# A transformer block with convolutional projections: the 3-tap convolution by minimal filtering, and a new order of the stages

## The chip, the cores and the metric

The kernel runs on one core of a Trainium2 chip. The metric is device time in microseconds. Five engines run at the same time, each on its own list of instructions in program order, and meet only at semaphores: TensorE (PE, matrix products into PSUM), VectorE (DVE), ScalarE (ACT), GpSimd (POOL, which here works on SBUF only) and SyncE (SP, which here issues nearly all DMA transfers).

## The reference, cut to what matters

The input x has 2 batches of 1024 tokens of 512 features. The block is an attention part and a feed-forward part (FFN), both with scale, shift and gate taken from a condition vector c.

```python
mod = (silu(c) @ wmod).reshape(2, 6, 1, 512)            # sa, ca, ga, sb, cb, gb
h = layernorm(x) * (1 + ca) + sa
y = conv1d(h, conv_w, taps=3, 'SAME') + conv_b          # 512 -> 3 * 128: thirds q, k, v
q, k, v = split(y, 3)                                   # in blocks of 128 tokens
qh, kh, vh = q @ wq + bq, k @ wk + bk, v @ wv + bv      # 16 heads of 64
o = softmax(causal(qh / 8 @ kh.T)) @ vh                 # within each block
x = x + ga * ((o @ wo + bo) @ proj_w + proj_b)
h = layernorm(x) * (1 + cb) + sb
x = x + gb * (h @ base_w.T + base_b + 0.5 * sum_over_top2_experts(weight * (h @ A.T) @ B))
```

The convolution for token t is g0 h[t-1] + g1 h[t] + g2 h[t+1], with g0, g1, g2 matrices of 512 x 384.

## The kernel before, in words

**Number format.** Every product runs in three passes over pairs of 16-bit halves: each operand is kept as a high half (the value rounded to float16) and a low half (what the rounding left), and PE adds high x high, high x low and low x high. So each operand that is made costs two operations: ACT writes the high half, then DVE or POOL writes the low half as value minus high half.

**Tiling.** The 2048 tokens are 8 chunks of 256 tokens (two blocks of 128). A chunk goes through these stages, named as in the list `SCHEDULE` as name:chunk:part. na and nb: mean, variance and normalisation of the input (statistics on DVE, the root in small steps on POOL, the scaling on DVE at L819). ht: PE transposes a block of 128 tokens x 512 features into a PSUM bank (L1065). hs: ACT and DVE take it out as high and low half into hT (L659, L824). halo: POOL copies the edge columns that the outer taps need from the chunk beside (L538). c: the convolution, a third (q, k or v) at a time, 36 matmuls of 256 tokens (L1167): 3 taps x 4 blocks of 128 features x 3 passes. When the last of them is done, ACT and DVE take the third out of PSUM with its bias as cv (L671, L898). qk and v: head projections (ACT L686, L697, DVE L907, L915). s: scores of 8 heads; m: their maximum on DVE (L921); e: exponential on ACT (L713); nz: normalisation on POOL (L587); ph: halves (ACT L722, DVE L927) and transposition by DMA; pv: product with v (oT on ACT L731, DVE L937). wo, pr: output projections and residual. l2a, l2b: second normalisation (xn, L970). hs2, lr, ro, rw: routing to experts. fb: base product; G and gh: routed activations (POOL L625; halves ACT L769, DVE L1020); fl: expert product and the result.

**Weights.** sp stages split weights. The convolution weights carry the factor (1 + ca), so they are split once per batch, in groups of four 128x384 operations on ACT (L647) and as many on DVE (L880): sp 0, 1, 2 for batch 0 and sp 11, 12, 13 for batch 1.

**The order.** `SCHEDULE` is one written list. Each engine walks it and issues its own part of every stage, so the list fixes the order within each engine and the waits do the rest. An instruction that waits holds back all that follow it on its engine, SP's transfers too. At the start SP issues the loads of x, of the modulation weights (wma, four parts), of the three thirds of the convolution weights (cw_raw) and of a projection weight (pw_raw), in this order on one queue. PE meanwhile computes the modulation: rp and row (L1081), its transposition cols (L1091), then vb (the convolution's bias, L1101), and then the convolution of chunk 0.

```python
tap, c, (a, b) = step // (3 * DC), step // 3 % DC, PASSES[step % 3]
ins = nc.tensor.matmul(bank_c[:, 0:CH], cw[:, i, a, c, tap, :],
                       hT[:, j % 2, b, c, OWN - 1 + tap:OWN - 1 + tap + CH],
                       start=step == 0, stop=step == STEPS - 1)
```

The same SBUF and PSUM are shared by all stages; three PSUM banks (C) serve ht, c, qk, v, pr and lr in turn.

Of the kernel before, what the change touches and what calls it, by code (L numbers as in the profile page):

```python
# [42 lines left out]
def bass_adaln_block(nc, x, cw_in, pw_in, wo_in, pj_in, bsw_in, btw_in, ar_in, small_in, pb_in, bb_in, wmod_in,  # L43
# [11 lines left out]
    STEPS = TAPS * DC * 3  # L55
    HALF = NC // 2
    S_SCALE = DH ** -0.5 / QK_SCALE ** 2
    assert W == P and D == 4 * P and 2 * DH == P and 2 * R == P and NC == 8 and CH == 2 * P
# [10 lines left out]
        hs:2:0 v:0:2 s:0:1 m:0:1 v:0:3 v:0:0 ph:0:0 c:1:3 pk:0:0 c:1:3 bias:0:0 c:1:3 ht:2:1 halo:2:0 c:1:3 e:0:1
        c:1:9 pj:0:1 nz:0:1 c:1:6 s:0:2 nb:3:0 m:0:2 c:1:3 hs:2:1 c:1:12 ph:0:1 cols:0:1 c:1:3 pk:0:1 c:1:6 e:0:2  # L70
        c:1:6 nz:0:2 c:1:15 qk:1:1 qk:1:0 xr:0:0 pv:0:0 qk:1:5 v:0:1 s:0:3 m:0:3 ph:0:2 qk:1:7 qk:1:4 c:1:3 na:4:0
        c:1:15 e:0:3 c:1:3 pick:0:2 c:1:12 nz:0:3 c:1:3 ht:3:0 hs:3:0 xr:1:0 qk:1:3 pv:0:1 qk:1:6 v:1:0 v:1:1 s:1:0
# [1259 lines left out]
```

## Time and profile before

| | us |
|---|---|
| timed runs | 458.02, 460.03, 460.16 (median 460.03) |
| profiled execution, first to last instruction (span) | 455.5 |
| median of the timed runs less that span | 4.5 |

| engine | busy us | share of the span | instructions |
|---|---|---|---|
| PE | 430.2 | 94% | 4284 |
| DVE | 364.4 | 80% | 695 |
| ACT | 303.0 | 67% | 976 |
| POOL | 250.6 | 55% | 301 |

The profile tells of one execution. Its own time is the span and what lies around it, which the profile does not show; beside the median of the timed runs that is 4.5 us. Times of instructions are from the span's start. The busy time of a pipelined engine holds the latency of the last operation of a series, so single durations (mean ns) add up to more than a series takes.

### The profile page before, as it was taken

To read this page: it belongs to the slowest core of one execution; us is meant where nothing else is said; L and a number is where in the kernel's file an instruction comes from. 1 tells how busy PE (TensorE), PEld (TensorE's weight loads), DVE (VectorE), ACT (ScalarE), POOL (GpSimd) and SP (SyncE) were. 2 spreads that over 40 slices of the span, in tenths; PEclk is the share of its full clock that TensorE was granted. 3 is DMA by queue.
4 is the path that set the end of the run, shared out by engine and by line. 5 is a ranking of instruction groups with operands and counts; after the bars stand their busy time and mean duration, and the time that the engine had idled before them with its cause. 6 is when DMAs were issued, how large, how long until landed. Compare 5 with 4: busy or idle time off the path is not lost.

```text
span 455.5 us, 11377 instructions
## 1 busy us (share of the span) xinstructions
PE 430.2 (94%) x4284; PEld 285.9 (63%) x4284; DVE 364.4 (80%) x695; ACT 303.0 (67%) x976; POOL 250.6 (55%) x301
## 2 busy tenths in 40 slices
PE   8799999999999998999999999979999898988996
PEld 6458578776887665576668765646675474454442
DVE  4879999999989899668976896568969986955751
ACT  2635888997987897566767687737777786541220
POOL 4103345321462877364675795535777779577471
PEclk9999999999999998999999999999999999999999
DMA  8994097232275298253891369353964563783642
GB/s 313 407 399 172 3 242 222 56 88 46 50 133 124 57 212 219 56 109 55 155 206 54 63 117 188 103 110 70 178 105 105 89 123 80 129 130 71 148 97 65
DMA packets 128006, 60.91 MB, mean 134 GB/s; under 512 B 117808, under 2 KB 118064, under 8 KB 127568
## 3 DMA queue, kind: packets, MB, share of 16 engines
q1 hardware_dynamic: 127808, 60.17, 56.1%
q8 instruction: 34, 0.56, 0.5%
q14 instruction: 20, 0.16, 0.1%
q10 hardware_dynamic: 144, 0.02, 0.1%
HBM read 26.63 MB, written 4.19 MB: 68 GB/s over the span
## 4 chain that ended last, share of the span: by engine, by line
PE 57%; DVE 20%; DMA 6%; POOL 6%; ACT 5%; issue 3%; SPq 2%; ACTq 0%; DVEq 0%; POOLq 0%
PE C L1167 15%; PE C L1037 12%; PE F L1037 11%; PE S L1213 4%; PE W L1230 3%; ACT prob L713 3%; PE W L1037 3%; DMA cw_raw<-in_cw_dram 3%; DVE xn L970 3%; DVE p L927 2%; PE S L1037 2%; DVE qk L907 2%; DVE nm L921 2%; DVE g L1020 2%; PE S L1205 2%
## 5 line engine op out<-in xcount | busy, mean ns | idle before, releaser
L587 POOL TENSOR_TENSOR prob<-prob,rinv 128x1024 f32<-128x1024 f32 x32 | 65.3, 2040 | 79.6 <-DVE rinv L932 79.5
L1167 PE MATMUL C<-hT,cw 128*128 128x256 f16 x864 | 108.0, 275 | 0.0
L1167 PEld LDWEIGHTS C<-hT,cw 128*128 128x128 f16 x864 | 82.4, 99 | 17.3 <-issue 2.6
L713 ACT ACTIVATE prob<-S,nms 128x128 f32<-128x128 f32 x256 | 90.1, 379 | 1.0
L1037 PE MATMUL F<-btw,gT 128*128 128x512 f16 x336 | 74.8, 379 | 0.0
L686 ACT ACTIVATE qk<-C,bqk 128x256 f16<-128x256 f32 x128 | 52.3, 481 | 21.1 <-PE C L1037 20.6
L907 DVE SCALAR_TENSOR_TENSOR qk<-C,bqk,qk 128x256 f16<-128x256 f32 x128 | 54.3, 474 | 10.5 <-ACT qk L686 10.4
L1037 PEld LDWEIGHTS F<-btw,gT 128*128 128x128 f16 x336 | 32.7, 98 | 38.0 <-DMA gT<-g 0.4
L713 ACT ACTIVATION_READ_ACCUMULATOR prob<-S,nms 128x1 f32 x256 | 55.7, 218 | 0.0
L1037 PE MATMUL C<-cv,pw 128*128 128x256 f16 x384 | 49.9, 273 | 3.5 <-DVE xb L948 3.1
L927 DVE SCALAR_TENSOR_TENSOR p<-prob,p 128x1024 f16<-128x1024 f32 x32 | 42.3, 1322 | 2.3 <-ACT p L722 2.2
L921 DVE TENSOR_REDUCE nm<-S 128x4 f32<-128x512 f32 x64 | 40.8, 678 | 3.4 <-PE S L1213 3.3
L1037 PEld LDWEIGHTS C<-cv,pw 128*128 128x128 f16 x384 | 35.9, 98 | 12.0 <-DVE xb L948 3.5
L1037 PE MATMUL F<-bsw,h 128*128 128x512 f16 x168 | 38.4, 379 | 0.9 <-DVE ob L1027 0.9
L722 ACT ACTIVATE p<-prob 128x1024 f16<-128x1024 f32 x32 | 34.0, 1062 | 2.0 <-DMA pt<-p 1.7
L625 POOL TENSOR_TENSOR G<-cmb,lr 128x1024 f32<-128x1024 f32 x15 | 30.1, 2005 | 2.0 <-DVE cmb L1011 1.7
L731 ACT ACTIVATE oT<-W 128x512 f16<-128x512 f32 x32 | 19.4, 607 | 15.2 <-PE W L1230 15.1
L1230 PE MATMUL W<-pt,v 128*64 128x128 f16 x768 | 27.5, 221 | 1.2 <-DVE oT L937 1.2
L631 POOL TENSOR_TENSOR xb<-xb,ob 128x512 f32<-128x512 f32 x12 | 16.5, 1379 | 21.8 <-DVE ob L1027 21.5
L1037 PEld LDWEIGHTS F<-bsw,h 128*128 128x128 f16 x168 | 16.0, 98 | 19.5 <-issue 1.3
L1230 PEld LDWEIGHTS W<-pt,v 128*64 128x64 f16 x768 | 22.4, 110 | 9.3 <-issue 6.8
L1213 PE MATMUL S<-qk 64*128 64x128 f16 x768 | 27.0, 217 | 0.0
(196 smaller groups left out, 756.6 us busy)
## 6 DMA issues: line engine op xcount, KB each, us to landing
xa<-in_x_dram SPq DMA_DIRECT2D x10, 512.0 KB, 4.9
xb<-in_x_dram SPq DMA_DIRECT2D x6, 512.0 KB, 4.1
wmb<-in_wmod_dram SPq DMA_DIRECT2D x1, 3072.0 KB, 19.1
out_dram<-xb SPq DMA_DIRECT2D x12, 256.0 KB, 2.5
cw_raw<-in_cw_dram SPq DMA_DIRECT2D x3, 768.0 KB, 10.6
raw<-in_cw_dram SPq DMA_DIRECT2D x3, 768.0 KB, 5.0
wma<-in_wmod_dram SPq DMA_DIRECT2D x4, 512.0 KB, 6.9
bt_raw<-in_btw_dram SPq DMA_DIRECT2D x2, 1024.0 KB, 5.7
```

The costliest lines, as they stand in the source:

```text
L587: nc.gpsimd.tensor_tensor(prob[:, i % 2], prob[:, i % 2], rinv[:, i % 2].unsqueeze(2).broadcast_to([P, 8, P]), ALU.mult).then_inc(p_normal, 1)
L625: nc.gpsimd.tensor_tensor(G_of(i), cmb[:, n].unsqueeze(2).broadcast_to([P, E, R]), lr[:, n, 0:R].unsqueeze(1).broadcast_to([P, E, R]), ALU ...
L686: nc.scalar.activation(qk16[:, HI, c], C[k][:, a * CH:(a + 1) * CH], ACT.Identity, bias=bqk[:, c:c + 1]).then_inc(c_hi, 1)
L713: ins = nc.scalar.activation(prob[:, i % 2, h], S[i % len(S)][h // 4][:, (h % 4) * P:(h % 4 + 1) * P], ACT.Exp, bias=nms[:, i % 2, h:h + 1 ...
L722: nc.scalar.activation(p16[:, HI], prob[:, i % 2], ACT.Copy, scale=P_SCALE).then_inc(p_hi, 1)
L907: ins = nc.vector.scalar_tensor_tensor(out=qk16[:, LO, c], in0=C[k][:, a * CH:(a + 1) * CH], scalar=bqk[:, c:c + 1], in1=qk16[:, HI, c], o ...
L921: ins = nc.vector.tensor_reduce(nm[:, i % 2, 4 * h:4 * h + 4], S[i % len(S)][h][:].rearrange("p (h k) -> p h k", h=4), AX.X, ALU.max, nega ...
L927: nc.vector.scalar_tensor_tensor(out=p16[:, LO], in0=prob[:, unit(j, n) % 2], scalar=P_SCALE, in1=p16[:, HI], op0=ALU.mult, op1=ALU.subtra ...
L1037: ins = nc.tensor.matmul(dst, stat(a), mov(b), start=first and i == 0, stop=last and i == 2)
L1167: ins = nc.tensor.matmul(bank_c[:, 0:CH], cw[:, i, a, c, tap, :], hT[:, j % 2, b, c, OWN - 1 + tap:OWN - 1 + tap + CH], start=step == 0, s ...
L1213: ins = nc.tensor.matmul(S[i % len(S)][h][:, q * P:(q + 1) * P], qk16[of_head, hi, c, b * P:(b + 1) * P], qk16[of_head, lo, NC + c, b * P: ...
L1230: ins = nc.tensor.matmul(w_bank(stage)[DH * h:DH * (h + 1), q * P:(q + 1) * P], v16[:, j % 2, hi, b, of_head], pt16[:, i % 2, lo, 4 * h + ...
```

## The change

Minimal filtering computes two neighbouring outputs of a 3-tap convolution with four products in place of six. A chunk's 256 tokens are now held as 128 pairs (even, odd). With e, o the even and odd token of a pair, o' the odd token of the pair before and e' the even one of the pair after, four inputs are made in float32, and four weights:

- inputs: t0 = o' - o, t1 = e + o, t2 = o - e, t3 = e' - e
- weights: g0, (g0 + g1 + g2) / 2, (g0 - g1 + g2) / 2, g2
- with product k = t_k times weight k, added over all features: even output = product 0 + product 1 + product 2, odd output = product 3 + product 1 - product 2. PSUM holds them as four regions of 128 columns.

New and changed stages:

- **sh** (SP): two DMA copies per chunk (and one row each at the seams between chunks) shift the neighbour tokens by one partition into place. **tz** zeroes the edges of a batch.
- **tt** (POOL): the four inputs, one 128x512 operation each, 32 in all. **halo** is gone (15 small operations).
- **ht/hs**: only chunks 0 and 1 still go through PE, with four transposes of 128x512 each. From chunk 2 on, **th** (ACT high half, DVE low half, 128x1024) and **tm** (one DMA transpose of 128x2048) turn two of the four inputs at a time: 12 of each.
- **wt** (POOL): the sums of the taps, three 128x512 operations for each third and batch (18). **sp** now splits taps 0 and 2 (128x256, groups of four), and new groups **sp 17 to 22** split the two sums (128x256).
- **c**: 48 matmuls of 128 columns per third in place of 36 of 256.
- **yv, y**: a third leaves PSUM by ACT (a copy of one region, and a copy with bias of another), DVE (add), POOL (add, subtract, 128x128 each), ACT (high half, 128x256 interleaved), POOL (low half).
- **lw, lm, ls, lt, lx, xl, rb** place SP's loads in the list as stages of their own.
- The whole list has a new order, with steps of 12 convolution matmuls.

```diff
-    STEPS = TAPS * DC * 3
+    NT = TAPS + 1
+    STEPS = NT * DC * 3
...
-        na:0:0 sil:0:0 nb:0:0 na:1:0 rp:0:0 ht:0:0 hs:0:0 ht:0:1 hs:0:1 row:0:0 nb:1:0 cols:0:0 ht:1:0 ht:1:1 sp:0:0
-        hs:1:0 hs:1:1 halo:0:0 halo:1:0 vb:0:0 c:0:27 sp:0:3 sp:0:1 vb:0:1 c:0:6 sp:0:4 c:0:12 sp:0:2 c:0:9 sp:0:6
...
+        sh:0:0 na:0:0 na:1:0 ht:0:1 ht:0:2 nb:0:0 rp:0:0 sh:0:1 nb:1:0 tz:0:0 sil:0:0 hs:0:1 hs:0:2 ht:0:0 row:0:0
+        ht:0:3 hs:0:0 cols:0:0 hs:0:3 sp:0:0 sp:0:3 tt:0:1 vb:0:0 c:0:12 sp:0:17 sp:0:1 wt:0:0 tt:0:2 sh:1:0 lw:0:0
+        tt:0:0 tt:0:3 sp:0:18 sp:0:4 wt:0:1 tt:1:1 tt:1:2 tt:1:0 vb:0:1 wt:0:2 c:0:48 na:2:0 yv:0:0 row:0:2 ht:1:0
...
+                elif s == "tm":
+                    sp.wait_ge(t16_lo, 2 * (j - EARLY) + n + 1)
+                    k, idx = bank(C_USE["c", j - 2, 2])
+                    sp.wait_ge(c_full[k], idx + 1)
+                    sp.dma_start_transpose(TT[:, j % 2, n].rearrange("p m t c q -> p (m t c) q"),
+                                           t16[:].rearrange("p m t d -> p (m t d)")).then_inc(t_moved[n], 16)
...
+                    elif n == 1:
+                        ins = nc.gpsimd.tensor_tensor(made, even, odd, ALU.add)
...
+                        pool.wait_ge(ld[f"cw{n}"], 16)
...
+                    link(nc.gpsimd.tensor_tensor(total, g[:, :, 0], g[:, :, 2], ALU.add))
+                    if n < 3:
+                        link(nc.gpsimd.tensor_tensor(plus, total, g[:, :, 1], ALU.add))
+                        nc.gpsimd.tensor_tensor(minus, total, g[:, :, 1], ALU.subtract).then_inc(wt_made, 1)
...
+                    nc.gpsimd.tensor_tensor(yb[:, use % 2, 0], yb[:, use % 2, 0], mb[:], ALU.add)
+                    nc.gpsimd.tensor_tensor(yb[:, use % 2, 1], yb[:, use % 2, 1], mb[:], ALU.subtract).then_inc(y_ready, 1)
+                elif s == "y":
+                    pool.wait_ge(cv_hi, Y_USE[stage] + 1)
+                    nc.gpsimd.tensor_tensor(halves(cv[:, n, LO]), yb[:, Y_USE[stage] % 2], halves(cv[:, n, HI]),
+                                            ALU.subtract).then_inc(cv_lo, 1)
...
+                    nc.scalar.activation(t16[:, HI], xt[:], ACT.Copy).then_inc(t16_hi, 1)
...
+                    nc.scalar.activation(mb[:], minus, ACT.Copy)
+                    if not spans(j):
+                        ins = nc.scalar.activation(yb[:, use % 2], plus.unsqueeze(1).broadcast_to([P, 2, P]), ACT.Identity,
+                                                   bias=col(0))
...
+                    nc.scalar.activation(halves(cv[:, n, HI]), yb[:, k % 2], ACT.Copy).then_inc(cv_hi, 1)
...
+                    nc.vector.tensor_tensor(t16[:, LO], xt[:], t16[:, HI], ALU.subtract).then_inc(t16_lo, 1)
...
+                    nc.vector.tensor_tensor(yb[:, use % 2], C[k][:, 0:2 * P].rearrange("p (b q) -> p b q", b=2),
+                                            yb[:, use % 2], ALU.add).then_inc(c_done[k], 1)
...
+                    pe.wait_ge(t_made, T_USE["tt", j, n] + 1)
...
-                    ins = nc.tensor.matmul(bank_c[:, 0:CH], cw[:, i, a, c, tap, :],
-                                           hT[:, j % 2, b, c, OWN - 1 + tap:OWN - 1 + tap + CH],
-                                           start=step == 0, stop=step == STEPS - 1)
+                    at = REGION[t] * P
+                    ins = nc.tensor.matmul(bank_c[:, at:at + P], cw[:, i, a, c, t, :], TT[:, j % 2, t // 2, b, t % 2, c, :],
+                                           start=step % (3 * DC) == 0, stop=step % (3 * DC) == 3 * DC - 1)
...
-                    c_wait(C_USE["c", j, i])
+                    pe.wait_ge(cv_lo, Y_USE["y", j, i] + 1)
```

## Rows read from the trace of the kernel before

**Rows 1.** Page, part 1: busy us, share of the span, instructions.

```profile
PE 430.2 (94%) x4284; PEld 285.9 (63%) x4284; DVE 364.4 (80%) x695; ACT 303.0 (67%) x976; POOL 250.6 (55%) x301
```

**Rows 2.** Page, part 4: the chain that ended last, by engine.

```profile
PE 57%; DVE 20%; DMA 6%; POOL 6%; ACT 5%; issue 3%; SPq 2%; ACTq 0%; DVEq 0%; POOLq 0%
```

**Rows 3.** Timeline of DVE: start us, us, operation; maxima 0:0, 3:0, 7:3.

```profile
45.53 1.28 DVE L921 TENSOR_REDUCE nm<-S 128x4 f32<-128x512 f32 x2
...
163.30 1.27 DVE L921 TENSOR_REDUCE nm<-S 128x4 f32<-128x512 f32 x2
...
381.36 1.29 DVE L921 TENSOR_REDUCE nm<-S 128x4 f32<-128x512 f32 x2 [0.35 <-PE S L1213]
```

**Rows 4.** Windows: stretch, length, busy us of each engine, clock, DMA.

```profile
0.00:15.50 15.50, 12.66 (x66) 9.02 (x66) 8.04 (x23) 3.14 (x6) 6.48 (x29) 1.00 0.88 342
15.50:45.50 30.00, 27.38 (x240) 20.05 (x241) 26.31 (x54) 17.31 (x36) 5.49 (x10) 1.00 0.81 314
45.50:163.30 117.80, 116.04 (x1350) 85.77 (x1348) 111.02 (x219) 101.56 (x339) 49.58 (x66) 1.00 0.46 107
163.30:381.40 218.10, 210.79 (x2203) 139.19 (x2202) 174.69 (x325) 158.67 (x543) 144.27 (x151) 0.99 0.59 119
381.40:455.50 74.10, 63.34 (x432) 31.85 (x430) 44.32 (x77) 22.35 (x57) 44.82 (x47) 1.00 0.52 104
```

**Rows 5.** Timeline: the start's modulation, and one routing group at 171 us.

```profile
8.05 1.91 PE L1081 MATMUL S<-wma,silw 128*32 128x512 f32 x8
...
9.89 1.09 PE L1065 MATMUL C<-ident,xa 128*128 128x128 f32 x8
...
13.70 0.43 PE L1091 MATMUL W<-ident,row_ab 64*128 64x64 f32 x4 [0.88 <-DVE row_ab L831]
...
14.55 0.28 DVE L838 COPY shift<-W 128x128 f32<-128x128 f32 x1
...
17.22 2.78 PE L1101 MATMUL F<-cw_raw,shift 128*32 128x384 f32 x24 [1.89 <-DMA cw_raw<-in_cw_dram]
...
18.28 1.06 ACT L647 ACTIVATE pw<-pw_raw 128x1024 f16<-128x1024 f32 x1 [0.25 <-DMA pw_raw<-in_pw_dram]
...
19.94 3.13 PE L1167 MATMUL C<-hT,cw 128*128 128x256 f16 x27
...
171.27 1.03 PE L1037 MATMUL C<-arw,h 128*128 128x80 f16 x24
```

**Rows 6.** Groups by form, DVE: xcount, busy us, mean ns, idle before.

```profile
L1020 DVE TENSOR_TENSOR g<-G,g 128x1024 f16<-128x1024 f32 x15 | 24.6, 1642 | 2.1 <-ACT g L769 1.9
...
L824 DVE TENSOR_TENSOR hT<-C,hT 128x512 f16<-128x512 f32 x14 | 9.4, 675 | 0.1
...
L898 DVE SCALAR_TENSOR_TENSOR cv<-C,cbias,cv 128x256 f16<-128x256 f32 x12 | 5.6, 464 | 2.4 <-ACT cv L671 2.3
```

**Rows 7.** Groups by form, ACT.

```profile
L722 ACT ACTIVATE p<-prob 128x1024 f16<-128x1024 f32 x32 | 34.0, 1062 | 2.0 <-DMA pt<-p 1.7 <-POOL prob L587 0.2
...
L671 ACT ACTIVATE cv<-C,cbias 128x256 f16<-128x256 f32 x12 | 5.8, 486 | 4.0 <-PE C L1167 4.0
```

**Rows 8.** DMA issues at 3.9 to 4.1 us: KB each, us to landing.

```profile
cw_raw<-in_cw_dram SPq DMA_DIRECT2D x1, 768.0 KB, 9.2
```

**Rows 9.** Groups by form, POOL.

```profile
L582 POOL TENSOR_TENSOR xb<-xb,gaPB 128x512 f32<-128x512 f32 x12 | 18.0, 1521 | 8.4 <-DMA xb<-in_x_dram 8.4
...
L615 POOL TENSOR_TENSOR cmb<-oh 128x32 f32<-128x32 f32 x7 | 2.5, 363 | 0.6
```

**Rows 10.** Four lines of DVE: count, duration ns min/median/max, first and last start.

```profile
L819 DVE TENSOR_SCALAR xa<-xa,mv,rs x16: 496/540/2122, 8.8 to 239.6; 128x512 f32<-128x512 f32 x16
...
L880 DVE SCALAR_TENSOR_TENSOR cw<-cw_raw,modT,cw x12: 607/610/617, 15.6 to 27.7; 128x384 f16<-128x384 f32 x12
...
L970 DVE TENSOR_SCALAR xn<-xb,mv,rs x12: 534/1546/2123, 123.3 to 357.7; 128x512 f32<-128x512 f32 x12
...
L1020 DVE TENSOR_TENSOR g<-G,g x15: 1193/1227/2965, 156.5 to 435.5; 128x1024 f16<-128x1024 f32 x15
```

More of the change, by code:

```diff
@@ L142, in bass_adaln_block, with latest @@
     CHI_USE = uses({"qk": 2, "v": 1})
+    T_USE = uses({"tt": 1})
+    Z_USE = uses({"tz": 1})
+    HS_USE = uses({"hs": 1})
+    Y_USE = uses({"y": 1})
+    TH_USE = uses({"th": 1})
+    PLACE = {stage: k for k, stage in enumerate(ORDER)}
+    def latest(stage, name):
+        return max((s for s in PLACE if s[0] == name and PLACE[s] < PLACE[stage]), key=PLACE.get, default=None)
     N_MOD = len(M_USE)
@@ L146, in bass_adaln_block @@
     C_COND = 3 + 3 * NC + 1
-    H_DONE = [2 * j + (2 if j == NCH - 1 else 1) for j in range(NCH)]
-    OWN, HW = 16, 288
+    EARLY = 2
+    REGION = (0, 2, 3, 1)
+    xpairs = x.rearrange("n (c p b) d -> (n c) p b d", p=P, b=2)
     xin = x.rearrange("n (c b p) d -> (n c) p b d", p=P, b=2)
@@ L173, in put @@
             return t
-        cw = put("cw", [P, 3, 2, DC, TAPS, P], F16)
+        cw = put("cw", [P, 3, 2, DC, NT, P], F16)
         pw = put("pw", [P, 3, 2, HE], F16)
@@ L207, in bass_adaln_block @@
         ffn_end = place[0]
+        h216_at = place[0]
+        h216 = put("h216", [P, 2, 2, D], F16)
+        t16 = put("t16", [P, 2, 2, D], F16, at=h216_at)
+        h216_end = place[0]
         gaPB = put("gaPB", [P, NB, D], F32)
@@ L324, in conv_split, with sums_split @@
         def conv_split(n, src, b, loaded):
-            return [(cw[:, n, HI, c], cw[:, n, LO, c], src[:, c], by_c(1, b)[c]) for c in range(DC)], loaded
+            return [(cw[:, n, HI, c, 0:NT:3], cw[:, n, LO, c, 0:NT:3], src[:, c, 0:TAPS:2], by_c(1, b)[c])
+                    for c in range(DC)], loaded
+        def sums_split(n, src, b, made):
+            return [(cw[:, n, HI, c, 1:3], cw[:, n, LO, c, 1:3], src(c), modH[:, c, b:b + 1]) for c in range(DC)], made
         def ffn_split(dst, src, b, loaded, first=0, count=DC):
@@ L346, in bass_adaln_block @@
                    ffn_split(arw, raw_ar, 1, (ld["raw"], 96))]
+        SUMS = len(SPLITS)
+        SPLITS += [sums_split(n, lambda c, k=n % 2: wt_raw[:, k, :, c], 0, (wt_made, n + 1)) for n in range(3)]
+        SPLITS += [sums_split(n, lambda c: raw_cw[:, c, 1:3], 1, (wt_made, n + 4)) for n in range(3)]
         M_BANK = {("row", 0, 0): S[0][0], ("cols", 0, 0): W[0], ("vb", 0, 1): F[1], ("pick", 0, 0): S[0][0],
@@ L377, in spans @@
         def spans(j):
-            at, to = (1 if j % CPB == 0 else 0), (CH - 1 if j % CPB == CPB - 1 else CH)
-            return [(0, at, to)] + [(1, 0, 1)] * at + [(2, CH - 1, CH)] * (CH - to)
+            whole, first, last = slice(0, P), slice(0, 1), slice(P - 1, P)
+            if first_of(j):
+                return [(0, slice(1, P), 0), (1, whole, 0), (0, first, 1)]
+            if last_of(j):
+                return [(0, whole, 0), (1, slice(0, P - 1), 0), (1, last, 2)]
+            return []
         def readers_of_third(j, i):
@@ L745, in _ @@
                             act.wait_ge(h2_moved[b], 16 * j)
+                        if (other := latest(stage, "th")) is not None:
+                            act.wait_ge(t_moved[other[2]], 16 * (other[1] - EARLY + 1))
                         nc.scalar.activation(h216[:, b, HI], xn2[:, b], ACT.Copy).then_inc(h2_hi, 1)
```

407 lines of the change are left out of this document (237 added, 170 removed).

## The prediction

> **What bounds the kernel now.** I read the busy shares first. PE is at 94%, DVE at 80%, ACT at 67%, GpSimd (POOL) at 55% [rows 1]. The chain of work that ended last is PE for 57% and DVE for 20% [rows 2]. A mean over stages can mislead, so I then cut the span at events that both orders share: 15.5 us, and the first maximum of the scores (stage m) of chunks 0 and 3 and the last one of chunk 7, at 45.53, 163.30 and 381.36 us [rows 3]. The table of those stretches [rows 4] is the base of everything below. I call them start (0 to 45.5), early (117.8 us), late (218.1 us) and tail (74.1 us).
>
> The reader is to see that early has two full engines: PE 116.0 and DVE 111.0 busy of 117.8. Late is PE's alone: 210.8 of 218.1, with DVE at 174.7. In the tail PE is busy 63.3 of 74.1. From 15.5 to 45.5 DVE is busy 26.3 of 30.0 (splitting weights), so it sets the pace there with PE. The change takes work from PE and gives work to DVE, ACT and GpSimd. So it can only gain late and in the tail, and pays in the start and early.
>
> **PE: what is saved.** Now a chunk takes 3 thirds x 36 = 108 convolution matmuls of 256 columns, later 3 x 48 = 144 of 128. Now 27 in a row take 3.13 us; less the 0.275 us that the last one trails, 110 ns a step [rows 5]. A 128-column matmul with a full weight load is not in the trace. Nearest below: 24 of 80 columns take 1.03 us, by the same count with 0.2 us 36 ns a step [rows 5]. Nearest above: the 110. By columns on the line between them, 128 gives 36 + 74 x 48/176 = 56 ns. I take that, since the 80-column row has the same weight load per matmul and still runs at 36. Whole kernel: 1152 x 56 = 64.5 us for 864 x 110 = 95.0, so -30.5 (ends 41.5 and 126.7 us). The transposes on PE fall from 64 to 32; 8 take 1.09 us [rows 5], so -4.
>
> By stretch, from the two lists of stages: early has 480 new steps for 348 old, 26.9 us for 38.3, and 28 transposes less. Late has 528 for 414, 29.6 us for 45.5, and 20 transposes less (-2.3): -18 together. Some 3 us of value and output groups lie behind the early border in the new list, so late and tail lose 15.
>
> **DVE.** In early, 7 th stages (low half of a 1024-wide half chunk) cost what the low half of G costs, 1.64 us each [rows 6]: 11.5. Three more groups of four weight splits come in. A split is 256 wide where the row has 384 at 0.61 us [rows 10], so between 0.41 and 0.61; I take 0.48: 12 x 0.48 = 5.8, and the four that were there get 0.5 cheaper. Seven hs at 0.675 go: -4.7. Ten yv adds at 0.464 stand for nine evacuations that cost no less: 0. Stages that cross the border (a normalisation in early that now comes later, one value group, one output) take 2.5 out. Sum +9.6, so 120.6 us busy. Low end: th at G's undisturbed 1.23 [rows 10], +6.7. At the present 94% early would last 128; at 99% with the low sum 119. I take 95%, as PE competes less: 127, **+9**. ACT gets close too: 7 th at 1.06, 10 yv of two operations of at most 0.49, 9 y at 0.49 and 12 splits at about that, less 9 cv at 0.49 and 7 hs between 0.49 and 1.06 [rows 7], some +18 on 101.6 of 117.8. So there is no slack elsewhere to buy this back.
>
> **The start.** Conv weights 0 land at 3.98 + 9.2 = 13.2 us [rows 8]. On GpSimd the new order is tt:0:1, wt:0:0, tt:0:2, tt:0:0, tt:0:3. The three tap sums of wt:0:0 wait for that landing. A two-input 128x512 operation takes 1.3 to 1.5 us there [rows 9], so tt:0:2 is made at about 13.2 + 3.9 + 1.3 = 18.4. PE stands in order with ht:0:2 ahead of rp, row, cols and vb: behind the blocked ht:0:2 waits the whole modulation, which now starts at 8.05 and has its cols at 13.70 us. From 18.4: ht 0.6, rp 1.9, ht 0.6, row 1.9, ht 0.6, row copy 0.7, cols 0.4, and 0.4 on DVE give 25.5; vb 2.8 more gives 28.3 for the first convolution, against 19.94 [rows 5]. The shifted copies (sh) are put on SP's queue behind the pw_raw load, which now lands at 18.3 [rows 5]; so about 19, just in time for ht:0:0. From the end of cols to the first maximum is now 30.5 us (15.0 to 45.5), DVE-bound. There DVE gets 12 sum splits (+5.8), cheaper old ones (-1.6), more hs (+2.4) and one qk and a product less (-2): +4.5. From 25.5 that gives 60.5 at DVE's present density and 56.5 with its gaps closed. I take 56.5, **+11**; ends +8 (only the shift of the first convolution) and +16.
>
> **Late and tail.** PE loses 15 of the two, taken whole: **-15**. GpSimd must stay off the path. Late it has 144.3 us. A 128-column operation lies between 0.36 (32 columns) and 1.5 (512) [rows 9], by columns 0.59; 256 gives 0.90. So 10 tt (15), 11 yv of two (13) and 12 y (11) make 183 of about 207: it fits, at 88%. DVE late gets about 11 and stands near 90%. With three engines there the ends are -20 (the present gaps shrink as well) and 0 (stalls eat it). The chain that a third now passes (two ACT copies, DVE, two GpSimd, ACT, GpSimd: about 0.9 + 0.5 + 1.2 + 0.5 + 0.9 = 4 us for 1 us) is hidden by the order wherever another chunk's stage stands between; uncovered it costs 3 us a third. Twelve half-chunk DMA transposes join 48 of the same size, behind others' waits on SP's queue. I count them at nothing while the queue stays under the 0.6 share that it has late [rows 4]; a late one holds back the next chunk's convolution for its landing.
>
> Sum: 455.5 + 11 + 9 - 15 = 460.5. The runs' median, 460.03, lies 4.5 above the span, so **465 us**.
>
> **A price that the sum holds only in part.** A normalisation (xn, nb) takes 0.50 to 0.54 us or up to 2.12 [rows 10]: 1.0 to 1.6 us longer when it falls beside a long GpSimd operation. The Trainium skill, GPSIMD Engine Reference, Specifications, says that GpSimd shares its SBUF interfaces with VectorE, against instructions in a two-port mode or with two SBUF inputs. By that rule splits, th and both normalisations would pay more as GpSimd's share grows, and the time would be that of the second rival below, worked out there from rows. The trace agrees for the normalisations; the first splits, beside an idle GpSimd, show nothing of it.
>
> **Rivals.**
>
> *The gain stands (faster).* Early, PE held DVE back as much as DVE held PE, so with PE light DVE runs at 99% on the low sum, 117.7, 119 us (+1); start +9; late and tail -15, and a third of PE's 18 us of gaps there goes, -6. Sum -11, **449 us**. For it: PE's 116.0 of 117.8 early. Against: 111.0 on DVE beside it leaves 6 us only, and the start. It decides if DVE's gaps early fall under 2 us.
>
> *GpSimd and DVE block each other (slower).* 122 more GpSimd operations, and 60 more exposed DVE ones (48 splits of the new kind, 12 th); at one us for every third of them, 20 us, of which three quarters fall where DVE is the bound: +15, **480 us**. It decides from about two such waits more per chunk. For it: half the xn are long already. Against: 12 of 12 first splits take 0.61.
>
> *Half the columns save nothing.* If a 128-column matmul cost 110 ns, the saving late turns into 528 x 54 ns = 28.5 us on the path: **493 us**. Against it: 36 ns at 80 columns.
>
> **How the numbers follow.** The forecast (break-even or somewhat slower) has 0.46, own range 454 to 475; the gain 0.30; the blocking 0.20; no saving 0.04. About 0.5% (2.3 us) is what a measurement can tell from no change. Of the forecast's 0.46, 0.05 lies below 457.7, 0.11 within, 0.30 above; of the gain 0.28 lies below and 0.02 within. So faster 0.33, same 0.13, slower 0.54. Eight in ten reach from 446 (into the gain) to 484 (past the blocking).
>
> **What would show it.** Conv matmuls 55 to 58 ns apart; first one at about 28 us; first maximum at 54 to 60; early 123 to 130 us with DVE over 93% and PE under 90%; late near 207, tail near 69. Wrong if the first maximum comes before 50 us, if early is no longer than now, or if PE is still over 95% busy early.

## The result, and the profile after

The changed kernel takes **612.76 us** (median of 4 runs, 610.98 to 613.63), the kernel before, beside it on the same chip, 460.1 us: a ratio of 1.331, with a 95% interval of 1.325 to 1.337. "Slower" was the likeliest side of the forecast, but the time lies 129 us above the top of the range. The profiled execution has a span of 611.3 us, against which the stretches below are summed.

The page of the kernel after, parts 1 and 4 (busy us and share of the span; then the chain that ended last, by engine and by line):

```profile
PE 444.3 (73%) x4540; PEld 284.0 (46%) x4540; DVE 397.6 (65%) x716; ACT 329.0 (54%) x1064; POOL 370.3 (61%) x407
...
DMA 18%; DVE 16%; POOL 13%; SPq 7%; PE 7%; issue 3%; ACT 3%; ACTq 0%; POOLq 0%; DVEq 0%
DMA xt<-xa 8%; DMA h<-h 3%; POOL prob L696 3%; PE S L1178 2%; DMA TT<-t 2%; DVE p L1068 2%; SPq L569 2%; DMA pt<-p 2%; DVE xn L1111 2%; DVE qk L1047 2%; DMA gT<-g 2%; DMA out_dram<-xb 1%; DVE nm L1062 1%; PE C L1178 1%; POOL G L734 1%
```

No engine is full now, where PE stood at 94% [rows 1], and PE has gone from 57% of the chain [rows 2] to 7%. First in the chain by line stands a DMA that the kernel before doesn't have: `xt<-xa`, the copies that shift neighbour tokens by one partition (sh). The same stretches as before, cut at the first score maximum of chunks 0 and 3 and at the last of chunk 7 (length, busy us of PE, weight loads, DVE, ACT, POOL, then granted clock, DMA share, GB/s):

```profile
0.00:15.50 15.50, 6.91 (x34) 6.35 (x34) 8.17 (x16) 1.49 (x2) 10.57 (x31) 0.81 0.87 348
15.50:87.30 71.80, 42.80 (x309) 24.72 (x310) 38.21 (x77) 26.39 (x61) 33.75 (x30) 0.76 0.23 78
87.30:270.80 183.50, 122.09 (x1450) 85.11 (x1449) 126.83 (x227) 111.78 (x369) 102.90 (x111) 0.83 0.71 128
270.80:537.40 266.60, 213.96 (x2386) 139.35 (x2385) 184.22 (x332) 171.85 (x582) 182.34 (x191) 0.92 0.63 112
537.40:611.30 73.90, 58.50 (x364) 28.46 (x362) 40.20 (x70) 17.54 (x50) 40.73 (x46) 0.95 0.47 96
```

Against [rows 4] the start is 41.8 us longer (87.3 for 45.5), early 65.7, late 48.5, and the tail, which holds no copies, is 0.2 shorter. DVE's and ACT's busy times early and late hardly differ from those of the kernels below that take 100 us less: the engines do not work longer, they wait. The granted clock of PE is lower as well. Early, with PE busy 122.1 of 183.5 us, its mean is 0.83 (between the two levels, 0.50 for 1.2 GHz and 1.00 for 2.4 GHz), where the kernel before has 1.00 at 116.0 of 117.8 us [rows 4]. In the kernel with the cut copies below it is 0.94, at 112.0 of 138.9 us. What the lower clock costs in all was not separated.

What they wait for shows in four views of the kernel after. First all issues of the copies on SP's queue (count, ns min/median/max; L522 and L530 copy 127 rows of 2 KB, L524 and L532 the one row at a seam behind them):

```profile
L522 SPq DMA_DIRECT2D xt<-xa x8: 602/662/1107, 9.6 to 383.2; - x8
L530 SPq DMA_DIRECT2D xt<-xa x8: 652/672/7096, 12.8 to 414.0; - x8
L532 SPq DMA_DIRECT2D xt<-xa x6: 3967/4116/9986, 19.9 to 359.7; - x6
L524 SPq DMA_DIRECT2D xt<-xa x6: 3902/4326/9316, 30.6 to 383.9; - x6
```

SP's queue in the start (start us, us held):

```profile
9.60 0.75 SPq L522 DMA_DIRECT2D xt<-xa  x1
12.78 7.10 SPq L530 DMA_DIRECT2D xt<-xa  x1
19.92 9.99 SPq L532 DMA_DIRECT2D xt<-xa  x1
29.95 0.62 SPq L522 DMA_DIRECT2D xt<-xa  x1
```

GpSimd's two inputs there that need a copy (in brackets what it waited, and for what):

```profile
28.20 1.26 POOL L640 TENSOR_TENSOR xt<-xt,xa 128x512 f32<-128x512 f32 x1 [9.96 <-DMA xt<-xa]
38.54 1.26 POOL L647 TENSOR_TENSOR xt<-xt,xa 128x512 f32<-128x512 f32 x1 [9.07 <-DMA xt<-xa]
```

A copy's own issue takes 0.66 us, but what is issued behind it is held 4 to 10 us. The first copy goes out at 9.60 and GpSimd has it at 28.2, where the prediction had "about 19"; the second has it 10.3 us later. One copy of 127 rows every 9.2 to 10.3 us is 72 to 81 ns a row, which looks like rows going one by one. From 30.5 to 37.5 us, with nothing but these copies under way, the 16 DMA engines are busy 7% on the mean and move 26 GB/s: about the work of one engine. In the first 15.5 us, with the loads, it is 87% and 348 GB/s. In the view of waits (us in total, times, longest) GpSimd loses 122 us to them:

```profile
POOL xt L647 <- DMA xt<-xa: 71.8, 7, 13.8
POOL xt L640 <- DMA xt<-xa: 50.2, 6, 10.5
```

The Trainium skill, DMA: Bandwidth & Descriptors, in "Why a DMA increments its semaphore by 16 and not by 1", says that a copy is spread over the largest number of DMA engines up to 16 that divides the length of the slowest dimension on both of its sides, and gives 127 partitions as a case that goes to a single engine. The 7% of above agrees with that, and so does the landing of the cut copies below, in 2.6 us.

### The profile page after: what moved, and what is told of

Read it like the earlier page. It is cut to its first block, busy times and chain, and to the rows that moved or that the text cites. A ratio compares the mean times of both kernels' runs of the same rounds, so it can differ in the third digit from the quotient of the medians.

```text
span 611.3 us, 12229 instructions
## 1 busy us (share of the span) xinstructions
PE 444.3 (73%) x4540; PEld 284.0 (46%) x4540; DVE 397.6 (65%) x716; ACT 329.0 (54%) x1064; POOL 370.3 (61%) x407
## 4 chain that ended last, share of the span: by engine, by line
DMA 18%; DVE 16%; POOL 13%; SPq 7%; PE 7%; issue 3%; ACT 3%; ACTq 0%; POOLq 0%; DVEq 0%
DMA xt<-xa 8%; DMA h<-h 3%; POOL prob L696 3%; PE S L1178 2%; DMA TT<-t 2%; DVE p L1068 2%; SPq L569 2%; DMA pt<-p 2%; DVE xn L1111 2%; DVE qk L1047 2%; DMA gT<-g 2%; DMA out_dram<-xb 1%; DVE nm L1062 1%; PE C L1178 1%; POOL G L734 1%
## 5 line engine op out<-in xcount | busy, mean ns | idle before, releaser
L1305 PE MATMUL C<-TT,cw 128*128 128x128 f16 x1152 | 77.9, 230 | 13.6 <-DMA TT<-t 8.3
L1305 PEld LDWEIGHTS C<-TT,cw 128*128 128x128 f16 x1152 | 72.1, 104 | 21.7 <-DMA TT<-t 8.6
L1178 PE MATMUL C<-cv,pw 128*128 128x256 f16 x384 | 59.1, 304 | 21.5 <-DVE qk L1047 7.1
L696 POOL TENSOR_TENSOR prob<-prob,rinv 128x1024 f32<-128x1024 f32 x32 | 68.1, 2129 | 10.3 <-DVE rinv L1073 10.1
L1068 DVE SCALAR_TENSOR_TENSOR p<-prob,p 128x1024 f16<-128x1024 f32 x32 | 48.4, 1513 | 18.1 <-ACT p L849 18.0
L1178 PEld LDWEIGHTS C<-cv,pw 128*128 128x128 f16 x384 | 38.7, 108 | 35.6 <-issue 20.9
L647 POOL TENSOR_TENSOR xt<-xt,xa 128x512 f32<-128x512 f32 x8 | 10.1, 1264 | 71.8 <-DMA xt<-xa 71.8
L1178 PE MATMUL C<-pw,cv 128*128 128x512 f16 x96 | 29.2, 425 | 29.1 <-DVE v L1056 18.5
L640 POOL TENSOR_TENSOR xt<-xt,xa 128x512 f32<-128x512 f32 x8 | 13.7, 1718 | 54.6 <-DMA xt<-xa 50.2
L774 ACT ACTIVATE t<-xt 128x1024 f16<-128x1024 f32 x12 | 12.7, 1060 | 55.3 <-POOL xt L647 18.4
L967 DVE TENSOR_TENSOR t<-xt,t 128x1024 f16<-128x1024 f32 x12 | 18.1, 1511 | 36.2 <-ACT t L774 36.2
L734 POOL TENSOR_TENSOR G<-cmb,lr 128x1024 f32<-128x1024 f32 x15 | 29.5, 1967 | 10.3 <-DVE g L1161 6.1
```

Of the source, the lines that this page charges most:

```text
L696: nc.gpsimd.tensor_tensor(prob[:, i % 2], prob[:, i % 2], rinv[:, i % 2].unsqueeze(2).broadcast_to([P, 8, P]), ALU.mult).then_inc(p_normal, 1)
L734: nc.gpsimd.tensor_tensor(G_of(i), cmb[:, n].unsqueeze(2).broadcast_to([P, E, R]), lr[:, n, 0:R].unsqueeze(1).broadcast_to([P, E, R]), ALU ...
L967: nc.vector.tensor_tensor(t16[:, LO], xt[:], t16[:, HI], ALU.subtract).then_inc(t16_lo, 1)
L1068: nc.vector.scalar_tensor_tensor(out=p16[:, LO], in0=prob[:, unit(j, n) % 2], scalar=P_SCALE, in1=p16[:, HI], op0=ALU.mult, op1=ALU.subtra ...
L1178: ins = nc.tensor.matmul(dst, stat(a), mov(b), start=first and i == 0, stop=last and i == 2)
L1305: ins = nc.tensor.matmul(bank_c[:, at:at + P], cw[:, i, a, c, t, :], TT[:, j % 2, t // 2, b, t % 2, c, :], start=step % (3 * DC) == 0, sto ...
```

## The experiments

Theory A: a 127-row copy runs on one DMA engine, and both its late landing and the hold on SP's queue cost the 108 us. Rivals: GpSimd and DVE block each other (B), the bytes (C), the seam copies (D), the smaller DMA scratch that the change also sets (R), the order of the stages (O). Ratios are against the kernel before, with 95% intervals.

### The copies

**Each copy cut in 112 and 15 rows.**

```diff
-                        sp.dma_start(t_of(j, 0)[1:P], own[0:P - 1]).then_inc(t_shifted[0][j % 2], 16)
+                        for lo, hi in ((0, 112), (112, P - 1)):
+                            sp.dma_start(t_of(j, 0)[lo + 1:hi + 1], own[lo:hi]).then_inc(t_shifted[0][j % 2], 16)
```

> The changed kernel with each copy of 127 rows issued as two: 112 rows and 15 rows, the same bytes. Theory A (a copy of 127 rows goes through one DMA engine, packet after packet, 10 us and more, and holds up the queue behind it): both parts land within about 3 us of their issue, GpSimd's wait for xt<-xa falls from 122 us to under 20, the one-row copies are issued in under 1.5 us, and the time comes down to 455 to 485 us. Rival B (GpSimd and DVE block each other, and the order of stages is bad; the copies are only where it shows): the landings may get shorter but the time stays over 550 us, with GpSimd and DVE operations as long as they are now. Rival C (any 127-row move between partitions is slow by its bytes, however it is cut): the time stays within 3% of 613 us and the two parts together still take 10 us.

Measured: **505.26 us**, 1.095 (1.088 to 1.102). The same bytes, 107.5 us less. The copies' issues in this kernel, with the time to landing:

```profile
L523 SPq DMA_DIRECT2D xt<-xa x16: 518/729/1340, 9.6 to 290.3; - x16
L532 SPq DMA_DIRECT2D xt<-xa x16: 528/847/1377, 12.8 to 314.0; - x16
...
L534 SPq DMA_DIRECT2D xt<-xa x6: 546/556/558, 14.2 to 275.7; - x6
L525 SPq DMA_DIRECT2D xt<-xa x6: 540/546/1571, 16.5 to 291.2; - x6
...
DMA to landing us min/median/max: 1.6/2.6/9.2
```

Its stretches early and late:

```profile
63.20:202.10 138.90, 111.99 (x1467) 79.61 (x1465) 128.64 (x227) 111.29 (x370) 107.36 (x106) 0.94 0.70 165
202.10:428.80 226.70, 203.09 (x2368) 134.85 (x2366) 186.03 (x331) 171.61 (x582) 183.44 (x194) 0.98 0.68 131
```

The signs of theory A come: a median landing of 2.6 us (9.2 at most), no issue over 1.6 us, and 12.2 us of waiting for the copies in all. But the time is 20 us above the expected top. Something else is left.

**128 rows without the shift.** Twelve copies become `sp.dma_start(t_of(j, 0), own)` with no seam row; the four at a batch's edge are cut.

> The changed kernel with 128 rows copied without a shift where it copies 127 rows shifted by one and one seam row (12 of 16 copies; the four at a batch's edge stay 127 rows, as 112 and 15). The first and last taps of the tokens are wrong by this. Theory A (127 does not divide among the 16 engines, 128 does): a copy of 128 rows lands in about 2 to 3 us and the time is that of the copy cut in two, within 1.5%. Rival C (a copy from SBUF to SBUF of 254 KB is slow by its bytes): 10 us a copy and 590 us or more. Rival D (what costs is the seam copy of one row, held 4 to 10 us at its issue): as theory A here, but then the kernel with the seam issued first must fall too.

Measured: 502.18 us, 1.090 (1.082 to 1.097), 0.6% from the cut copies. One row more, and one DMA instead of two, does what the cut does. C falls.

**The seam row issued first**, the two `dma_start` calls swapped.

> The changed kernel with the one-row seam copy issued before the copy of 127 rows, nothing else. Theory A: the 127-row copy still goes packet after packet and lands 10 us after issue, and what stands behind it on SP's queue (the next transposes and loads) is held in place of the seam copy: 590 to 620 us. Rival D (the seam copies themselves hold the queue, by their own small packets): their issue falls under 1 us, nothing else is held, and the time falls under 540 us.

Measured: 618.9 us, 1.344 (1.337 to 1.352). SP's queue in its start:

```profile
12.86 7.05 SPq L531 DMA_DIRECT2D xt<-xa  x1
19.95 0.64 SPq L532 DMA_DIRECT2D xt<-xa  x1
20.63 9.19 SPq L523 DMA_DIRECT2D xt<-xa  x1
29.87 0.61 SPq L524 DMA_DIRECT2D xt<-xa  x1
30.52 9.95 SPq L482 DMA_DIRECT2D pw_raw<-in_pw_dram  x2
```

The hold moves to whatever stands behind a 127-row copy (L524, L532), here a weight load. D falls.

**No copies at all** (both differences made from unshifted tokens, `sh` issues nothing).

> The changed kernel with no shift copies at all: the first and the fourth difference of tokens are made from the unshifted even and odd tokens, at the same place and of the same size, so the first and fourth product are wrong. It shows what all the copies cost. Theory A: 450 to 475 us, and within 3% of the copy cut in two, since parts that go through 16 engines land in time. Rival B (GpSimd and DVE blocking, the order): over 550 us even so. If it is 2 to 5% below the cut copies, these still cost as transfers or as waits of SP's queue.

Measured: 492.74 us, 1.069 (1.063 to 1.074): outside what A expected. The cut copies still cost 12.5 us, 8 of them late (226.7 against 218.5 us). And 32 us over the kernel before stay with no copy in it.

**The scratch alone**, on the kernel before: `dynamic_dma_scratch_size=512`.

> The kernel before with the one part of the change that the prediction did not speak of: dynamic_dma_scratch_size=512 in the line that sets up the program. Theory A (the one-engine copies are the whole reason for the difference between the changed kernel and the cut copies): 457 to 463 us, no change. Rival R (a smaller scratch throttles the queues; then the holds of 4 to 10 us on SP's queue come from it, not from the copies): SP's DMA issues take longer than 0.7 us here too and the time is 470 us or more.

Measured: 459.05 us, 0.995 (0.991 to 1.000). R falls; the kernels below that start from the one before have this setting.

**Sixteen idle copies in the kernel before**, one at each ht stage, into a buffer that nobody reads, of 127 rows; and the same cut.

```diff
+                if s == "ht":
+                    i = 2 * j + n
...
+                    for lo, hi in ((0, P - 1),):
+                        sp.dma_start(idle[lo + 1:hi + 1, 1 + i % 6], idle[lo:hi, 0]).then_inc(idle_moved[i % 6], 16)
```

> The kernel before, with that scratch and 16 copies of 127 rows of 2 KB more on SP's queue, at the 16 ht stages, into a buffer that no engine reads: nobody waits for them until the end. Theory A: each still runs about 10 us on one engine and what comes behind it on the queue (transposes, loads) is late: 475 to 530 us. Rival W (what the changed kernel lost was only GpSimd's wait for the landing): 456 to 466 us.

> As the kernel with 16 idle copies, but each cut in 112 rows and 15 rows, the same bytes. Theory A: 457 to 466 us, each lands in 3 us. If copying itself (bytes, or two more issues on SP's queue) costs, it is within 2% of the uncut one.

Measured: 553.05 us, 1.204 (1.194 to 1.213), and cut 466.96 us, 1.013 (1.006 to 1.019), 1 us over what A expected. Nobody waits for these copies, and uncut they cost 93 us. SP's queue of the uncut one:

```profile
14.15 26.43 SPq L460 DMA_DIRECT2D idle<-idle  x4
40.62 11.05 SPq L427 DMA_DIRECT2D pw_raw<-in_pw_dram  x2
...
101.74 0.63 SPq L460 DMA_DIRECT2D idle<-idle  x1
102.50 4.53 SPq L448 DMA_DIRECT2D xa<-in_x_dram  x1
...
108.30 11.39 SPq L485 DMA_TRANSPOSE pt<-p  x1
```

Four in a row hold the weight loads to 40.6 us: the start takes 89.0 us for 45.5. Later a single copy delays the transposes of the products: one is held 11.39 us at its issue, where the longest in the kernel before takes 3.76. So the hold alone is enough for most of such a loss; how the 108 us of the changed kernel divide between hold and GpSimd's own wait was not separated.

### What is left: 45 us

**A new order in the start**, on the cut copies: `wt:0:0` behind the token sums, `row:0:0` and `cols:0:0` ahead of `ht:0:0`.

> The kernel with the cut copies, and in the stage list the first tap sums (wt:0:0) behind the four token sums on GpSimd, and row:0:0 and cols:0:0 ahead of ht:0:0 (PE and DVE). By the prediction's step for the start (PE stands behind ht:0:2, which stands behind the tap sums): rp starts at about 14 us in place of 19.4, the first convolution at 23 to 26 in place of 30.2, the first maximum 4 to 7 us earlier than 63.2 us, the time 497 to 502 us. Rival (the start is bound by DVE's splits and the chain through ACT, DVE and GpSimd behind the convolution): first maximum at 61 us or later, 503 to 507 us.

Measured: 509.8 us, 1.105 (1.098 to 1.111): 4.5 us worse, and 3 us over the rival's range. PE did nearly what was expected (first convolution at 26.45 for 30.16 us), but the first maximum came at 68.1 for 63.2. DVE's splits show why, first with the old order, then with the new one, where GpSimd's sums of taps and tokens run beside them:

```profile
27.94 2.74 DVE L1026 SCALAR_TENSOR_TENSOR cw<-cw_raw,modT,cw 128x256 f16<-128x256 f32 x4
32.21 1.66 DVE L1026 SCALAR_TENSOR_TENSOR cw<-wt_raw,modH,cw 128x256 f16<-128x256 f32 x4
33.79 1.66 DVE L1026 SCALAR_TENSOR_TENSOR cw<-cw_raw,modT,cw 128x256 f16<-128x256 f32 x4
```

```profile
24.70 5.50 DVE L1026 SCALAR_TENSOR_TENSOR cw<-cw_raw,modT,cw 128x256 f16<-128x256 f32 x4
32.80 3.22 DVE L1026 SCALAR_TENSOR_TENSOR cw<-wt_raw,modH,cw 128x256 f16<-128x256 f32 x4
35.94 4.69 DVE L1026 SCALAR_TENSOR_TENSOR cw<-cw_raw,modT,cw 128x256 f16<-128x256 f32 x4
```

Three groups of four take 13.4 us in place of 6.1. What PE gained, DVE paid back. The same meeting can go the other way. In the old order a tap sum falls beside the group at 33.79 us: there the splits keep their 0.42 us each, and GpSimd's sum takes 5.29 us, where the undisturbed one takes 1.26:

```profile
34.01 5.29 POOL L664 TENSOR_TENSOR wt_raw<-cw_raw 128x512 f32<-128x512 f32 x1 [4.40 <-DVE cw L1026]
```

No run shows what decides which of the two is held.

**GpSimd's narrow sums left out** (of the two sums of yv one goes and one is made one column wide; y has full width in chunk 0 only).

> The kernel with the cut copies; GpSimd's two sums behind the convolution (yv) are one column wide, and the low half (y) is made full width in the first chunk only, so most values are wrong: some 50 us of GpSimd's 376 us go, all other engines do the same. Theory B (what is left over the forecast is GpSimd's new work, by its queue and by DVE's operations that it lengthens): 475 to 488 us, DVE's time of the products' low halves (p) falls towards 1.25 us from 1.51. Rival (DVE's and ACT's own new work sets the time): 498 us or more.

Measured: 503.29 us, 1.090 (1.084 to 1.096). GpSimd's busy time falls from 376 to 345 us, 31 of the 50 expected, and the time by 2, with overlapping intervals of the ratios. DVE's p takes 1.55 us and did not fall. B fails here, for these operations.

**th's low half as a fill**, `nc.vector.memset(t16[:, LO], 0.0)`.

> The kernel with the cut copies; the low half of the token sums that go to the DMA transposes (th on DVE, 12 operations of 1.46 us) is a fill with zeros, so the low products are wrong. If DVE is the bound early, as the prediction had it: 12 us less DVE work give 491 to 498 us, most of it in the stretch from the first maximum to that of chunk 3. If GpSimd or the queue is: 502 us or more.

Measured: 494.23 us, 1.071 (1.065 to 1.077). DVE's busy time falls by 12.2 us and the time by 11.0, so DVE is on the path. By stretch of the profiled executions (8.7 us apart), early gets 3.0 us shorter for 4.6 us less of DVE and late 4.7 for 7.8, where early was expected to have most. So about six tenths of DVE's work come off, early as late.

**All of these together**: no copies, narrow sums, the fill, the new start.

> No shift copies, no full sums behind the convolution on GpSimd, zeros for th's low half, and the new start order, together (the output is wrong by all of these): what the cheaper convolution gives if the work that came with it is mostly gone. The prediction's late and tail term (-15 us where PE alone is the bound): 430 to 448 us, late under 207 us. Rival (half as many columns save nothing on the path): 455 us or more.

Measured: 482.64 us, 1.046 (1.039 to 1.053). A miss, on the rival's side: still 21 us slower. Late, at 216.3 us, is nearly as long as before (218.1):

```profile
189.50:405.80 216.30, 200.31 (x2371) 133.16 (x2370) 176.05 (x331) 170.43 (x582) 164.38 (x183) 0.99 0.69 132
```

Of what remains over the kernel before, the start holds 14.6 us (first maximum at 60.1) and early 11.4. Not all the added work is gone here: GpSimd's 50 wide sums (32 of tokens, 18 of taps), DVE's 24 more splits, ACT's copies and the 12 transposes by DMA are all still there. No run took the wide sums out of the changed kernel.

**Is PE the bound late?** One of three passes left out (288 of 864 convolution matmuls, 31.7 us), on the kernel before; then on the cut copies.

```diff
                     i, step = n
+                    if step % 3 == 1:
+                        continue
```

> The kernel before without one of the three passes of its convolution (high half of the weights by low half of the data: 288 of 864 matmuls of 110 ns, 31.7 us of PE), all other work and the order as they are; the output lacks that pass. The prediction's step (late and tail are PE's alone, so PE work taken away there comes off whole): late falls from 218 to 205 us or less, by about the 15 us that go there, and the time is 435 to 446 us. Rival O (late is shared: the stages stand in an order in which DVE, ACT, GpSimd and the transposes end the waits as often as PE): late 211 us or more and the time 449 us or more.

> The kernel with the cut copies, without the same pass of its convolution (384 of 1152 matmuls of 56 ns, 21.5 us of PE); the output lacks that pass. If PE still bounds the changed kernel late: 485 to 493 us. Rival O (PE is off the path in the changed kernel): 499 us or more.

Measured: 449.19 us, 0.980 (0.971 to 0.989), and 501.01 us, 1.090 (1.080 to 1.099). The stretches of the kernel before, early and late, without that pass:

```profile
44.90:160.60 115.70, 104.01 (x1223) 73.04 (x1218) 110.32 (x220) 101.49 (x341) 50.21 (x66) 1.00 0.47 109
160.60:371.40 210.80, 196.92 (x2069) 125.82 (x2068) 174.23 (x324) 157.57 (x540) 143.60 (x150) 0.99 0.60 123
```

Late loses 138 matmuls, 15.2 us, and gets 7.3 us shorter (218.1 before); PE's idle time there goes from 7.3 to 13.9 us. This is what the prediction took to come off whole. On the changed kernel 21.5 us of PE are worth 4 by the times and 2 by the ratios, whose intervals overlap. Late, where some 10 us of matmuls go, PE's busy time falls by 7.0 us (its granted clock is 0.96 for 0.98) and the stretch by 2.9. Nearest to rival O. (449 us is below both kernels, but by doing a third less of the convolution's products; no version of the changed kernel came down to the one before.)

**Idle GpSimd work in the kernel before**, of about the added amount: two 128x512 sums at each ht stage, two 128x128 and one 128x256 behind each third. Then the same without the pass; then the wide ones alone; then these with one input (`tensor_scalar`) in place of two.

```diff
+                if s == "ht":
...
+                        ins = nc.gpsimd.tensor_tensor(idle[:, 1 + i], idle[:, 0], idle[:, 3], ALU.add)
...
+                elif s == "c" and n[1] == STEPS - 1:
+                    nc.gpsimd.tensor_tensor(idle[:, 4, 0:P], idle[:, 0, 0:P], idle[:, 3, 0:P], ALU.add)
```

> The kernel before, with that scratch and idle GpSimd work of about the amount that the change adds, where the change has it: two 128x512 operations at each of the 16 ht stages, two 128x128 and one 128x256 at the end of each of the 24 convolution thirds; nobody reads the results. The prediction's step (GpSimd fits beside the rest): 457 to 464 us, DVE's operations as long as before. The prediction's rival (GpSimd and DVE block each other): DVE's busy time rises by 10 us or more and the time is 472 to 490 us.

> The kernel before with the idle GpSimd work (486.5 us) and without the one pass of the convolution: the change's two main sides, less PE and more GpSimd, on the old order. If they add up, the time is 486.5 less what the missing pass alone gains, about 462 us by the prediction's step. If GpSimd's work and what it lengthens has become the bound: 478 us or more, and the gain on PE is lost here too.

> The kernel before with only the 32 wide operations of the idle GpSimd work (two of 128x512 with two inputs at each ht stage), without the 72 narrow ones behind the convolution. If the wide ones are what costs (the changed kernel gained next to nothing when its narrow sums were left out): 475 to 487 us, and DVE's busy time stays 12 us or more over the 364 of the kernel before. If the narrow ones do, or the cost goes by GpSimd's busy time: 46 of some 94 us are left, so 470 us or less.

> The same 32 idle operations of 128x512 with one input tensor (scale and shift by constants) in place of two. If it is the second input in SBUF that holds DVE up: DVE's busy time within 4 us of the kernel before, and 459 to 468 us (what is left is GpSimd's own occupancy). If any wide GpSimd operation does: as with two inputs, within 1%.

Measured: 486.54 us, 1.055 (1.049 to 1.062); without the pass 484.81, 1.052 (1.039 to 1.064); wide ones alone 472.84, 1.032 (1.025 to 1.040); with one input 458.31, 1.000 (0.995 to 1.006). First with all idle work, then wide alone, then one input: the idle group where it is read, and DVE's first 12 splits. (The last one's profile is of an execution of 464.25 us, so no stretch is read from it.)

```profile
L562 POOL TENSOR_TENSOR idle<-idle 128x512 f32<-128x512 f32 x32 | 46.8, 1483 | 0.6
...
L894 DVE SCALAR_TENSOR_TENSOR cw<-cw_raw,modT,cw 128x384 f16<-128x384 f32 x12 | 11.7, 1030 | 0.8 <-ACT cw L661 0.8
```

```profile
L562 POOL TENSOR_TENSOR idle<-idle 128x512 f32<-128x512 f32 x32 | 46.3, 1468 | 0.4
...
L890 DVE SCALAR_TENSOR_TENSOR cw<-cw_raw,modT,cw 128x384 f16<-128x384 f32 x12 | 11.7, 1039 | 0.7 <-ACT cw L657 0.7
```

```profile
L562 POOL TENSOR_SCALAR idle<-idle 128x512 f32<-128x512 f32 x32 | 21.5, 687 | 0.4
...
L890 DVE SCALAR_TENSOR_TENSOR cw<-cw_raw,modT,cw 128x384 f16<-128x384 f32 x12 | 7.7, 698 | 0.8 <-ACT cw L657 0.8
```

Work that nobody reads costs 26 us, a little more than the 20 of the rival, and eats PE's gain (1.7 us left of 9.6). Nine of the 26 lie in the start (54.7 for 45.5 us), where eight idle sums stand on GpSimd's queue ahead of the halo columns that the first convolution needs. The wide ones alone end between the two expectations, so the narrow ones cost 10 to 14 (by the ratios or by the times). By stretch of the profiles, the wide ones alone cost 9.2 us in the start, 4.9 early and nothing late (217.7 for 218.1 us); all of them cost 9.2, 13.0 and 7.9. The splits go from 0.61 us [rows 10] to 1.03 beside two-input sums and 0.70 beside one-input operations of the same shape, which cost nothing in all. DVE's busy time is 379.6 us with the wide two-input sums and 369.5 with one input, for 364.4 [rows 1]; within 4 was expected of the latter. The one-input operations also take half as long on GpSimd, and in the start the halo columns come at 28.0 us behind the wide two-input sums (the first convolution waits 8.1 us for them) and at 20.8 behind these, for 18.5 before, so occupancy and conflict are not fully told apart.

## Why the prediction was wrong

**The step that failed** is "the shifted copies (sh) are put on SP's queue behind the pw_raw load [...] so about 19, just in time for ht:0:0": 16 copies got the landing of a neighbouring load and no price. They measured 107.5 us over the cut ones. With the copies cut the step is right to the tenth: GpSimd makes its first input that needs one at 19.31 us. The prediction weighed the transposes on that queue and passed by the copies; it never asked how 127 rows divide, nor what stands behind a copy. No rival held it.

That leaves 505 against 465. In spans, 503.0 against 460.5, the miss of 42.5 us is, by its own terms:

- **Conv at 56 ns: right.** 48 in a row take 2.85 us late with the cut copies, 0.22 of it the trailing one:

```profile
304.25 2.85 PE L1307 MATMUL C<-TT,cw 128*128 128x128 f16 x48
```

- **Start +11: +17.7 measured** (63.2 us). The shift of the modulation was right but for 1.9 us (first convolution at 30.16 us for 28.3). Nearly all of these are rp, taken from [rows 5] at 1.91 us for 8 matmuls: PE had stood idle for 9.9 of the 12 us before, and the first 8 of its 16 ran at a granted clock of 0.50:

```profile
19.38 3.63 PE L1223 MATMUL S<-wma,silw 128*32 128x512 f32 x8
```

Closing DVE's gaps behind it was not right: the other end, 60.5, was nearer, and the new start order shows a second bound behind it, DVE beside GpSimd's sums. (The lower end of "1.3 to 1.5 us" for a wide GpSimd operation stands in no line of [rows 9]; the undisturbed sums took 1.26.)
- **Early +9: +21.1.** DVE is the fullest engine, busy 128.6 of 138.9 us (93%; 95% taken), but the mechanism, time by DVE's busy time alone, held only in part: of 4.6 us taken from it there, 3.0 came off. Its busy time was mis-sized by 8.0. The groups behind that are shown here, first p in the kernel before, then early with the cut copies (count, busy us, mean ns). The two cw groups are the 16 splits of batch 1 there, taken at 0.48:

```profile
L927 DVE SCALAR_TENSOR_TENSOR p<-prob,p 128x1024 f16<-128x1024 f32 x11 | 13.3, 1213 | 0.5 <-ACT p L722 0.5
```

```profile
L1070 DVE SCALAR_TENSOR_TENSOR p<-prob,p 128x1024 f16<-128x1024 f32 x11 | 16.2, 1470 | 1.1 <-ACT p L851 1.1
...
L1026 DVE SCALAR_TENSOR_TENSOR cw<-raw,modH,cw 128x256 f16<-128x256 f32 x8 | 7.9, 1044 | 0.0
...
L1026 DVE SCALAR_TENSOR_TENSOR cw<-raw,modT,cw 128x256 f16<-128x256 f32 x8 | 6.4, 864 | 0.2 <-ACT cw L758 0.2
```

The splits are 6.6 us over 16 x 0.48, and p, not priced at all, is at 1.47 us for 1.21, 2.8 more. th was 1.46 for 1.64. The 0.48 came from splits beside an idle GpSimd; early they take 0.86 to 1.04. That GpSimd's sums do this is shown for the start, by the new order there; for early, and for p, it is argued.
- **Late and tail -15: +8.7.** "Late is PE's alone", read from 97% busy, failed: PE work taken from the kernel before is worth half there, and next to nothing beside the added GpSimd work. With the cut copies PE is busy 11.5 us less in late and tail, and none of it came off. The cut copies add 8; without any, late is 218.5 us, the 218.1 of before:

```profile
197.90:416.40 218.50, 198.97 (x2354) 130.48 (x2352) 185.72 (x331) 170.64 (x582) 185.87 (x194) 0.99 0.68 130
```

GpSimd's busy time was right (183.4 us for 183). That it fits beside the rest was not, in the kernel before: idle work that brings it to 176.7 us late costs 7.9 there.
- **Transposes by DMA at nothing: right** once the queue is free: with the cut copies the view of waits lists none for them (TT<-t) early and one of 5.1 us late, though the queue's share late is 0.68, over the 0.6 that was the condition.
- **The blocking rival** (480 us) named a mechanism that is there, and idle work costs the kernel before as much (486.5), nine of the 26 us in the start. It stands beside the lost gain on PE and the later start; its own part of the 45 us was not isolated in the changed kernel.

Which waits keep late at 216 us with much of the added work gone stays open; that it is the order of the stages is argued from the runs without a pass, not shown by one that changes the order there, and the wide sums that stay are a rival that no run removed (idle ones alone cost the kernel before nothing late). Why leaving out the narrow sums gained 2 us where idle ones cost 10 to 14 is open too.

## What to carry to other kernels

Look at the row count of every DMA that a change adds, and cut one like 127 (here into 112 and 15): bytes do not tell its price, and everything behind it on the queue pays as well. An engine that is 97% busy in an in-order schedule is not thereby worth its time: take work away from it and see, before counting a saving. DVE, 93% busy early, gave back 3.0 us of 4.6. A duration from a stretch where GpSimd is idle is a lower end for the same operation beside GpSimd's two-input sums.

## What the hardware showed

- A 127-row copy of 254 KB takes 9.2 to 10.3 us in a row of them, with 7% of the 16 DMA engines busy, and holds up the next DMA of its queue; 128 rows, or 112 and 15, land in about 3 us (medians 3.0 and 2.6).
- DVE splits of 0.42 us each (1.66 for four) take 1.38 (5.50) beside GpSimd's two-input sums, or keep their time and hold the sum up (5.29 us for 1.26). Beside one-input operations of GpSimd the splits lengthen much less (0.70 us, beside two-input sums 1.03, alone 0.61). The Trainium skill, GPSIMD Engine Reference, Specifications, says that GpSimd shares its SBUF interfaces with VectorE, with contention against VectorE instructions in a two-port mode or with two SBUF inputs. The trace now agrees for the splits, which the prediction said it did not show.
